# Layer normalisations of a post-norm decoder: scaling on GpSimd instead of VectorE, and new slots

## What is computed

```python
def _layernorm(x, axis=-1, eps=1e-05):
    m = jnp.mean(x, axis=axis, keepdims=True)
    v = jnp.var(x, axis=axis, keepdims=True)
    return (x - m) / jnp.sqrt(v + eps)

x = _layernorm(x + _L0_attn_ref(...))    # 8 heads of 128, one K and V for all
x = _layernorm(x + _L0_xattn_ref(...))   # 16 heads of 8, causal
x = _layernorm(x + _L0_ffn_ref(...))     # 8 experts, two chosen, gated by silu
x = _layernorm(x + _L1_attn_ref(...))    # windows of 64
x = _layernorm(x + _L1_xattn_ref(...))
x = _layernorm(x + _L1_ffn_ref(...))     # 8 linear experts, two chosen
x = _layernorm(x + _L2_attn_ref(...))    # rotary, causal
x = _layernorm(x + _L2_xattn_ref(...))   # 16 heads of 64
x = _layernorm(x + _L2_ffn_ref(...))     # quantised; scales over all of x
x = _layernorm(x + _L3_attn_ref(...))
x = _layernorm(x + _L3_xattn_ref(...))   # normalises its inputs again, with gain and bias
x = _layernorm(x + _L3_ffn_ref(...))     # normalises its input again, silu
```

## Time and profile before

| | |
|---|---|
| median of three runs | 1844.06 us |
| profiled execution: its own time | 1848.42 us |
| its span, first to last instruction | 1846.6 us |
| mean granted TensorE clock | 0.952 |
| TensorE busy, matmuls | 1656.5 us, 90% |
| VectorE busy | 1430.0 us, 77% |
| ScalarE busy | 1213.6 us, 66% |
| GpSimd busy | 738.9 us, 40% |
| last normalisation of a part, L0_attn to L2_xattn (us from the start) | 170, 298, 503, 613, 736, 825, 958, 1148 |
| the same, L2_ffn to L3_ffn | 1282, 1434, 1817, 1844 |

### The profile page before, as it was taken

How to read it: one execution, slowest core, us unless ns; L and a number is a source line. 1 busy time by engine, 2 the same in 40 slices (tenths; PEclk the granted TensorE clock), 3 DMA queues, 4 the chain that set the end, 5 groups by cost and what they waited for, 6 DMA issues and landing times. The chain is left out here.

```text
span 1846.6 us, 41706 instructions
## 1 busy us (share of the span) xinstructions
PE 1656.5 (90%) x14731; PEld 1218.2 (66%) x14793; DVE 1430.0 (77%) x3949; ACT 1213.6 (66%) x4785; POOL 738.9 (40%) x928
## 2 busy tenths in 40 slices
PE   8999999999999897789999997618988999999998
PEld 7886558989755565246678886315556766777667
DVE  5666886777889998988857776878997777777765
ACT  3447996655699995149954443636986767666675
POOL 2235871000266884137720000025765444344446
PEclk9999999999978999789999999759999999999999
DMA  9000000000000000000000000100000000000000
GB/s 294 1 1 2 2 2 1 2 2 1 2 2 2 2 2 2 1 1 2 2 2 2 2 2 31 80 0 1 1 2 1 1 1 1 1 1 1 1 1 24
DMA packets 11678, 22.28 MB, mean 12 GB/s; under 512 B 5200, under 2 KB 8528, under 8 KB 10832
## 3 DMA queue, kind: packets, MB, share of 16 engines
q1 hardware_dynamic: 11472, 19.61, 3.3%
HBM read 18.55 MB, written 1.05 MB: 11 GB/s over the span
## 5 line engine op out<-in xcount | busy, mean ns | idle before, releaser
L1692 POOL TENSOR_TENSOR a_probs<-a_probs,a_rinv 128x512 f32<-128x512 f32 (+1 forms) x288 | 271.8, 945 | 178.5 <-DVE a_rinv L1525 174.9
L1315 ACT ACTIVATE a_probs<-bank,a_negmax 128x128 f32<-128x128 f32 x896 | 326.1, 439 | 20.5 <-DVE a_negmax L1494 20.4
L1692 POOL TENSOR_TENSOR c_probs<-c_probs,c_rinv 128x512 f32<-128x512 f32 x192 | 200.1, 1042 | 210.1 <-DVE c_rinv L1525 206.9
L1728 POOL TENSOR_TENSOR a_rstd<-a_ve,neg_half 128x1 f32<-128x1 f32 x128 | 70.2, 548 | 516.3 <-DVE a_ve L1583 515.6
L1315 ACT ACTIVATION_READ_ACCUMULATOR a_probs<-bank,a_negmax 128x1 f32 x896 | 240.1, 279 | 0.0
L1112 PEld LDWEIGHTS bank<-const,a_probs 128*128 128x128 f32 x1024 | 117.2, 145 | 111.9 <-issue 91.6
L1112 PE MATMUL bank<-const,a_probs 128*128 128x128 f32 x1024 | 176.2, 291 | 0.9 <-DVE a_probs_t L1532 0.9
L1494 DVE TENSOR_REDUCE a_negmax<-bank 128x4 f32<-128x512 f32 x224 | 151.9, 679 | 22.7 <-PE bank L1083 18.0
L1532 DVE COPY a_probs_t<-bank 128x512 f32<-128x512 f32 (+1 forms) x192 | 118.4, 617 | 26.4 <-PE bank L1112 26.3
L1094 PE MATMUL bank<-state_t,w_L_ffn 128*128 128x128 f32 x1024 | 137.0, 277 | 0.0
L1313 ACT ACTIVATE c_probs<-c_probs,c_negmax 128x256 f32<-128x256 f32 x256 | 126.9, 502 | 0.0
(11 more groups left out here) (269 smaller groups left out, 4418.0 us busy)
## 6 DMA issues: line engine op xcount, KB each, us to landing
w_L_ffn<-in_L_ffn SPq DMA_DIRECT2D x1, 3184.0 KB, 20.2
w_L_xattn<-in_L_xattn SPq DMA_DIRECT2D x1, 2050.0 KB, 8.7
w_L_attn<-in_L_attn SPq DMA_DIRECT2D x3, 512.0 KB, 5.7
w_L_xattn<-in_L_xattn SPq DMA_DIRECT2D x1, 1536.0 KB, 8.7
ctx_t<-in_ctxT SPq DMA_DIRECT2D x1, 1024.0 KB, 12.1
ctx<-in_ctx SPq DMA_DIRECT2D x1, 1024.0 KB, 11.8
out<-state SPq DMA_DIRECT2D x16, 64.0 KB, 1.6
state_t<-in_xT SPq DMA_DIRECT2D x1, 768.0 KB, 8.7
```

The source lines that it names most:

```text
L1315: op = act.activation(p, bank_of("scores", n)[:, j * width:(j + 1) * width], ACT.Exp, bias=negmax[:, n % PB, j:j + 1], accum_out=rsum[:, n ...
L1692: pool.tensor_tensor(p, p, along(rinv[:, n % PB, 0:heads], wide(kind) // heads), ALU.mult).then_inc(sems["norm_done"], 1)
L1728: pool.tensor_tensor(rstd[:, b:b + 1], ve[:, b:b + 1], neg_half[:, 0:1], ALU.pow).then_inc(sems["rstd_ready"], 1)
```

## The change

Epsilon, power and subtraction with scaling of every normalisation (the first, the second and that of the context) are now three linked instructions of GpSimd in slot "normalise" ("normalise_again"); `var_ready` is raised by `bn_aggr`. On VectorE `add_and_stats` is cut into `sum_up`, `parts` (`bn_stats`) and `moments` (`bn_aggr`). The sum stands at the head of a slot, `bn_stats` behind the first "max" unit, `bn_aggr` behind the first "back" unit. The statistics of the second normalisation get a slot of their own ("again"). Before VectorE writes a sum into `R` it waits until the slot's former state is normalised (`sum_free`), since that is now read by GpSimd. Many numbers of the tables change. The diff, cut (the table lines of `max`, `front` and others are whole):

```diff
-    "h8": [("qk", 10, "act"), ("v", 5, "dve")],
+    "h8": [("qk", 10, "act"), ("v", 4, "dve")],
...
-    "h8r": [("qk", 9, "dve"), ("v", 6, "dve")],
-    "moe": [("router", 26, "dve"), ("gateT", 6, "act"), ("biases", 2, "dve")],
+    "h8r": [("qk", 9, "dve"), ("v", 7, "dve")],
+    "moe": [("router", 27, "dve"), ("gateT", 4, "act"), ("biases", 2, "dve")],
...
-    "scores": {"all": 3, "h8": 6, "h8p": 6, "h8r": 6, "moe": 4, "h64c": 4, "h64m": 6, "ffn": 4},
-    "max": {"all": 3, "h8": 6, "h8p": 5, "h8r": 6, "h64c": 4, "h64m": 5, "ffn": 4},
-    "front": {"all": 3, "h8": 5, "h8p": 4, "h8r": 5, "lin": 2, "h64c": 3, "h64m": 4},
-    "norm": {"all": 2, "h8": 4, "h8p": 3, "moe": 1, "ffn": 3},
-    "second": {"all": 0, "h64c": 1},
-    "back": {"all": 0, "h8r": -1, "ffn": -1},
-    "values": {"all": -1, "h8": -2, "h8p": -2, "h8r": -2, "h64c": 1},
-    "outs": {"all": -1, "h8": -2, "h8p": -2, "h8r": -2, "h64c": 1, "lin": -2, "ffn": -2},
+    "scores": {"all": 3, "h8": 6, "h8p": 6, "h8r": 6, "moe": 6, "h64c": 4, "h64m": 6, "ffn": 4},
+    "max": {"all": 3, "h8": 7, "h8p": 5, "h8r": 7, "h64c": 4, "h64m": 5, "ffn": 4, "moe": 5},
+    "front": {"all": 3, "h8": 5, "h8p": 4, "h8r": 5, "lin": 2, "h64m": 4, "moe": 5},
+    "norm": {"all": 2, "h8": 4, "h8p": 3, "moe": 1, "ffn": 3, "h8r": 3},
+    "second": {"all": 0, "h64c": 1, "lin": -2, "moe": -1, "mqa": 1},
+    "back": {"all": 0, "h8r": -1, "ffn": -1, "mqa": 1},
+    "values": {"all": -1, "h8": -2, "h8p": -2, "h8r": -2, "h64c": 1, "mqa": 0},
+    "outs": {"all": -1, "h8": -2, "h8p": -2, "h8r": -2, "h64c": 1, "lin": -2, "ffn": -2, "mqa": 0},
...
-    "output": {"all": 3, "mqa": 2, "h64c": 1, "down": 5},
-    "stats": {"all": 3, "mqa": 2, "h64c": 1, "lin": 4, "h64m": 4, "down": 5},
-    "normalise": {"all": 5, "mqa": 3, "h8": 4, "moe": 6, "h64c": 3, "h64m": 6, "ffn": 6, "down": 7},
-    "normalise_again": {"all": 6, "mqa": 5, "h8p": 7, "moe": 8, "h64m": 7, "ffn": 4},
-    "turn": {"all": 6, "mqa": 5, "h8p": 7, "moe": 7, "h64c": 5, "h64m": 7, "down": 8},
-    "take": {"all": 6, "mqa": 5, "h8p": 7, "moe": 7, "h64c": 5, "h64m": 7, "ffn": 8, "down": 8},
+    "output": {"all": 3, "mqa": 2, "h64c": 1, "down": 4, "lin": 2},
+    "stats": {"all": 3, "mqa": 2, "h64c": 1, "lin": 4, "h64m": 4, "down": 4},
+    "normalise": {"all": 5, "mqa": 3, "h8": 3, "moe": 6, "h64c": 3, "h64m": 6, "ffn": 6, "down": 6, "h8r": 4, "lin": 4, "h8p": 4},
+    "again": {"all": 6, "mqa": 4, "h8": 5, "moe": 7, "h64c": 4, "ffn": 7},
+    "normalise_again": {"all": 6, "mqa": 5, "h8p": 7, "moe": 8, "h64m": 7, "ffn": 4, "h8r": 7},
+    "turn": {"all": 6, "mqa": 5, "h8p": 7, "moe": 8, "h64c": 5, "h64m": 7, "down": 9, "h8": 8, "h8r": 8},
+    "take": {"all": 6, "mqa": 5, "h8p": 7, "moe": 8, "h64c": 5, "h64m": 7, "ffn": 8, "down": 9, "h8": 8, "h8r": 8},
...
-            parts.append("normalise_again")
+            parts += ["again", "normalise_again"]
...
+                            sum_free(dve, s)
...
-                        link(dve.bn_stats(st6[:, b, :], R[:, b % R_RING, :]))
-                        link(dve.bn_aggr(mv[:, b, :], st6[:, b, :]))
-                        dve.tensor_scalar(ve[:, b:b + 1], mv[:, b, 1:2], EPS, None, ALU.add).then_inc(sems["var_ready"], 1)
-
-                    def normalise(s):
+                        chain[0] += 1
+                        parts_done[s] = chain[0]
+                        dve.bn_stats(st6[:, b, :], R[:, b % R_RING, :]).then_inc(sems["chain_dve"], 1)
...
+                    def moments(s):
+
                         b = plan.steps[s][1]
-                        dve.wait_ge(sems["rstd_ready"], s + 1)
-                        dve.tensor_scalar(X[:, b, :], R[:, b % R_RING, :], mv[:, b, 0:1], rstd[:, b:b + 1], ALU.subtract, ALU.mult).then_inc(sems["x_ready"], 1)
-                        if plan.affine_next(s):
-                            dve.wait_ge(sems["x_ready"], s + 1)
-                            link(dve.bn_stats(st6b[:, b, :], X[:, b, :]))
-                            link(dve.bn_aggr(mv2[:, b, :], st6b[:, b, :]))
-                            dve.tensor_scalar(ve2[:, b:b + 1], mv2[:, b, 1:2], EPS, None, ALU.add).then_inc(sems["stat2_ready"], 1)
-
-                    def normalise_again(s):
+                        dve.wait_ge(sems["chain_dve"], parts_done[s])
+                        dve.bn_aggr(mv[:, b, :], st6[:, b, :]).then_inc(sems["var_ready"], 1)
...
-                        dve.wait_ge(sems["rstd2_ready"], 1 + sum(plan.affine_next(t) for t in range(s)))
-                        dve.tensor_scalar(LH[:, b % R_RING, :], X[:, b, :], mv2[:, b, 0:1], rstd2[:, b:b + 1], ALU.subtract, ALU.mult).then_inc(sems["norm2_ready"], 1)
...
                        for what, s in plan.after.get(n, []):
+                            if what == "stats" and plan.kind(s) in PROJECTED:
+                                sum_up(s)
+                            if what == "normalise" and not last_loop and plan.next_kind(s) is None:
+                                ffn["state_max"](dve, plan.steps[s][1], sems["x_ready"], s + 1)
+                        for what, s in plan.after.get(n, []):
+                            if what == "again":
+                                parts_again(s)
+                        for m in plan.due["max"].get(n, [])[:1]:
+                            front(m)
+                        for what, s in plan.after.get(n, []):
                             if what == "stats":
-                                add_and_stats(s)
-                            if what == "normalise":
-                                normalise(s)
-                                if not last_loop and plan.next_kind(s) is None:
-                                    ffn["state_max"](dve, plan.steps[s][1], sems["x_ready"], s + 1)
-                            if what == "normalise_again":
-                                normalise_again(s)
-                        for m in plan.due["max"].get(n, []):
+                                parts(s)
+                        for m in plan.due["max"].get(n, [])[1:]:
                             front(m)
-                        for m in plan.due["back"].get(n, []):
+                        for m in plan.due["back"].get(n, [])[:1]:
                             back(m)
+                        for what, s in plan.after.get(n, []):
+                            if what == "stats":
+                                moments(s)
+                            if what == "again":
+                                moments_again(s)
+                        for m in plan.due["back"].get(n, [])[1:]:
+                            back(m)
+                        for s in plan.context.get(n, []):
+                            context_moments(s)
...
-                            if what == "stats":
+                            if what == "normalise":
                                 pool.wait_ge(sems["var_ready"], s + 1)
-                                pool.tensor_tensor(rstd[:, b:b + 1], ve[:, b:b + 1], neg_half[:, 0:1], ALU.pow).then_inc(sems["rstd_ready"], 1)
-                            if what == "normalise" and plan.affine_next(s):
+                                link(pool.tensor_scalar(ve[:, b:b + 1], mv[:, b, 1:2], EPS, None, ALU.add))
+                                link(pool.tensor_tensor(rstd[:, b:b + 1], ve[:, b:b + 1], neg_half[:, 0:1], ALU.pow))
+                                pool.tensor_scalar(X[:, b, :], R[:, b % R_RING, :], mv[:, b, 0:1], rstd[:, b:b + 1], ALU.subtract, ALU.mult).then_inc(sems["x_ready"], 1)
+                            if what == "normalise_again":
                                 pool.wait_ge(sems["stat2_ready"], 1 + sum(plan.affine_next(t) for t in range(s)))
-                                pool.tensor_tensor(rstd2[:, b:b + 1], ve2[:, b:b + 1], neg_half[:, 0:1], ALU.pow).then_inc(sems["rstd2_ready"], 1)
+                                link(pool.tensor_scalar(ve2[:, b:b + 1], mv2[:, b, 1:2], EPS, None, ALU.add))
+                                link(pool.tensor_tensor(rstd2[:, b:b + 1], ve2[:, b:b + 1], neg_half[:, 0:1], ALU.pow))
+                                pool.tensor_scalar(LH[:, b % R_RING, :], X[:, b, :], mv2[:, b, 0:1], rstd2[:, b:b + 1], ALU.subtract, ALU.mult).then_inc(sems["norm2_ready"], 1)
                         for s in range(len(plan.steps)):
                             if plan.first[s] - 3 == n:
                                 if plan.layer(s).out_bias:
```

34 lines of the change are left out of this document (24 added, 10 removed).

## The result

The changed kernel takes 1870.5 us (median of 4; 1866.8 to 1871.8) against 1843.9 for the kernel before, measured beside it: ratio 1.0142, 95% interval 1.0124 to 1.0159. I had said 1825 (1802 to 1854): wrong in sign and outside the range, 45 us too low. The profiled execution took 1869.6 us, its span is 1867.7.

What follows compares the result with a forecast made beforehand. TensorE, ScalarE or VectorE was taken as the bound by layer, with L0_ffn waiting for gates. Terms -10 - 5 - 7 - 1 - 1 + 5 gave -19 us from the 1844.1 median: 1825, range 1802 to 1854.

Steps and rivals of the forecast that it cites:

- L0_ffn, -10: Moved slots of L0_ffn: TensorE's 0.7 us wait for the chosen gates goes in 14 batches, gain 10 us.
- The price of a normalisation on GpSimd, 1.2 us: Epsilon, power and subtraction on GpSimd take 1.2 us from start to start, ends 1.1 and 1.7.
- The end, +5: In L3_ffn GpSimd becomes the bound, 2.1 us a batch against 1.72; loss 5 us, 3 to 13.
- L3_attn, -7: L3_attn: VectorE loses 1.3 of 8.3 busy us a batch, period 8.1; 7 us gained with the mixed stretch, ends 0 and 13.
- L1_xattn, hidden until 1.75 us: In L1_xattn GpSimd's added work, 6.7 of 7.22 us a batch, costs nothing until one normalisation costs 1.75.
- L3_xattn, nothing: In L3_xattn the long 1.07 us subtraction is VectorE's own time beside a full TensorE: no gain.
- L1_ffn, -5: L1_ffn: VectorE saves 0.5 us of 5.2 a batch over 12 batches; gain 5 us, ends 0 and 9.
- L1_attn and the down projection, -1 each: L1_attn and the down projection, alternating with the start of L3_attn, gain 1 us each, ends -2 and +3.
- L2_attn and L2_xattn, no step at all: Both layers were taken as full on TensorE, where taking work from VectorE buys nothing; no term in the sum.
- Rival 3: Slower by GpSimd's price, 2.2 us a normalisation: L1_xattn +7, L3_attn +13, end +21; +24 in all, 1868 us; chance 0.16.
- two short links: L1_ffn: the two links around the aggregate, with other work now in them, estimated at 0.1 us each a batch.

## Why the prediction was wrong

From -19 to +21, by the profiled spans, is 40 us. Two things failed: the price of a normalisation on GpSimd, and the waits for its result, which the sum put at nothing. With the measured price of 1.76 my own sum gives 14 for the end and 0 for L3_attn, -3 in all, 1841: the price alone doesn't turn the sign. By the steps of the prediction:

- **L0_ffn, -10: right.** -10.4; the wait of the earlier trace rows is gone, and the slots alone do it (-11.2).
- **The price of a normalisation on GpSimd, 1.2 us: this step failed.** It is 1.76, above my upper end. I chose 0.33 for the subtraction by the row of a byte mask with two constants, because both are scalar operations, and so took even the two-input addition of 0.455 for the upper end; epsilon on 128x1 is 0.23, not 0.15. The line that I drew for the fixed part (0.13) joined this byte row to a float32 row of 2048 elements; float32 rows don't lie on it: 0.23 us for 1 element, 0.62 to 0.81 for 128, 2.79 for 2048. The Trainium skill, "GPSIMD Engine Reference" (introduction), has VectorE roughly twice as fast in ordinary elementwise arithmetic, and I had set that against the row; measured, it is 0.81 against 0.34 us, 2.4 times. The price that I had worked out by it, 1.7 with 13 us at the end, was much nearer than the one I took.
- **The end, +5: right mechanism, mis-sized by that price.** My own sum with 1.76 gives the last state at 1819.5 + 10.5 + 16 x 1.76 = 1858.2, +14; measured +14.9. A starting pair (0.95) and a normalisation (1.76) are 2.71 us of GpSimd, and the period is 2.72.
- **L3_attn, -7: nearly the size, wrong reason.** -10.2, but the slots alone give -11.3 with no relief of VectorE, so the number came near by luck. My sum for GpSimd, 6.2 - 1.1 + 2 x 1.2 = 7.5, is 8.6 with the measured price: the bound that I had looked for in ScalarE.
- **L1_xattn, hidden until 1.75 us: right, at the edge.** GpSimd is at 94%; the layer takes 119.5 to 124.1 us in the six traces with this code, 122.8 before.
- **L3_xattn, nothing: failed.** I read the subtraction as VectorE's own time beside a full TensorE, and didn't ask who waits for its result. The second statistics stand in the slot of the normalisation that they read, 4.6 us a batch behind GpSimd, and TensorE stands 1.2 us a batch for the second normalised state that follows from them: +15.6 us. With these steps one slot later it is 382.1 us, under the 383.3 of before.
- **L1_ffn, -5: the gain is real and was blocked.** I took off VectorE's 0.5 us and didn't follow the state from GpSimd to the turn that the second matmuls of the next batch stand behind. With the turn later the period is 4.58, against my 4.7; as built it is 5.83. The layer is only 1.2 us longer, since its last seven batches got shorter (40.3 to 35.3 us). In the old code the same relief took only 2.2 us off the layer.
- **L1_attn and the down projection, -1 each:** +0.4 (less than L1_attn's own scatter) and +2.8; what costs the 2.8 wasn't tried.
- **L2_attn and L2_xattn, no step at all:** +3.2 and +4.0. L2_attn's period is 7.86 with VectorE subtracting and 8.38 with GpSimd, where TensorE waits 0.8 us a batch for the exponentials. Of L2_xattn's 4.0 us 2.8 are at its entry: its first batch comes 9.94 us behind the last of L2_attn instead of 7.16. It comes later (9 to 11 us) in every version that has the new slots or the new code, and not with L0_ffn's slots alone. What causes this wasn't tried.

The miss of 40 us is 9.9 at the end, 15.6 in L3_xattn, 11 in L2, 6.2 in L1_ffn, and about -3 in all others. By layers the price explains a quarter, the end. L3_xattn and L1_ffn, 22 us, are waits for GpSimd's result. The 11 us of L2 stay open, but for L2_attn's longer period with GpSimd's subtraction. Rival 3 had 1868 us, but not by what happened: it put the price at 2.2 and the loss into L1_xattn and L3_attn. And the part of the change that I counted as a single step, the statistics between the units, I priced at two short links; with VectorE still subtracting it costs 65 us (1824.0 to 1889.6).

## What to carry to other kernels

Price an operation on another engine from a row with the same data types and operands on that engine, and where none is, keep the far end in the range. Then follow the result of the moved work to every reader, and check for each whether it stands in an in-order queue within the new latency; the losses in L3_xattn and L1_ffn went when the readers moved by one and by two slots. And take a change with several parts apart before believing any of them: here the slots alone gave -20 us, the rest +46.
